# Sums and weighted values of a block's last four heads, issued in two pairs instead of all four at once

## What is computed

```
x = x + block0(group_norm(x))    # q, k, v: 3x3 depthwise convolution, layer norm per head
x = x + block1(group_norm(x))    # q, v get a low-rank term; no convolution
# in each block, for each of 12 heads of 16 channels, over 256 tokens:
attn = q @ k.T / 4 + rel_h[:, :, :, None] + rel_w[:, :, None, :]   # (256, 256)
o    = softmax(attn) @ v         # block0: + q before the output projection
out  = o @ w_proj + b_proj
```

## Time and profile before

| | |
|---|---|
| median of 3 runs | 108.78 us (107.95 to 112.67) |
| the profiled execution's own time | 108.68 us |
| its span, first to last instruction | 106.7 us |
| TensorE matmul busy | 97.1 us (91%) |
| TensorE weight loads busy | 70.8 us (66%) |
| VectorE busy | 62.7 us (59%) |
| ScalarE busy | 51.3 us (48%) |
| GpSimd busy | 31.4 us (29%) |

### The profile page before, as it was taken

One profiled execution on the slowest core, in us unless ns is written; L12 is line 12 of the kernel. 1 busy time (PEld: TensorE's weight loads), 2 busy tenths in 40 slices (PEclk: granted clock), 3 DMA queues, 4 the chain that ended last, 5 costly groups with the idle time before them and its releaser, 6 DMA issues.

```text
span 106.7 us, 2097 instructions
## 1 busy us (share of the span) xinstructions
PE 97.1 (91%) x822; PEld 70.8 (66%) x825; DVE 62.7 (59%) x134; ACT 51.3 (48%) x115; POOL 31.4 (29%) x46
## 2 busy tenths in 40 slices
PE   5799999999959999999999999899989999999780
PEld 2155787578848986777856563797759879857440
DVE  3469995587999667834650135464796493560130
ACT  4011904663534981837815624254246668715820
POOL 8947600599999999000000000000000000000000
PEclk9995579999999999999999999999999999999999
DMA  2999980000000000000000000000000000000002
GB/s 59 308 307 292 237 79 0 3 0 6 0 0 0 9 0 0 0 0 6 0 0 0 0 6 0 0 0 0 0 0 6 0 0 6 0 0 0 0 0 74
DMA packets 2826, 3.73 MB, mean 35 GB/s; under 512 B 305, under 2 KB 2242, under 8 KB 2818
## 3 DMA queue, kind: packets, MB, share of 16 engines
q0 software_dynamic: 784, 0.79, 6.7%
q1 hardware_dynamic: 1282, 1.41, 4.8%
q10 hardware_dynamic: 752, 1.42, 4.5%
HBM read 3.42 MB, written 0.20 MB: 34 GB/s over the span
## 4 chain that ended last, share of the span: by engine, by line
PE 75%; DVE 10%; ACT 7%; DMA 3%; issue 2%
PE bank L917 9%; PE bank L760 8%; PE bank L853 6%; PE bank L850 6%; PE bank L749 6%; PE bank L892 5%; PE bank L905 5%; PE bank L866 5%; PE bank L893 4%; PE bank L831 3%; ACT pt L386 3%; DVE taps_m L622 3%; DMA x<-x_t 3%; PE bank L734 3%; PE bank L832 2%
## 5 line engine op out<-in xcount | busy, mean ns | idle before, releaser
L575 DVE TENSOR_REDUCE mx<-bank 128x2 fp32r<-128x512 f32 x24 | 15.0, 682 | 3.2 <-PE bank L866 3.2
L386 ACT ACTIVATE pt<-bank 128x512 f32<-128x512 f32 x24 | 13.0, 594 | 3.6 <-PE bank L893 3.4
L892 PE MATMUL bank<-qs,ks 128*128 128x256 f32 x48 | 13.3, 310 | 0.8 <-ACT pt L386 0.7
L570 DVE SCALAR_TENSOR_TENSOR qs<-qs,vec,bank 64x512 fp32r<-64x512 f32 x12 | 8.8, 737 | 6.9 <-ACT qs L376 6.8
L893 PE MATMUL bank<-mt,nhot_r 128*128 128x256 f32 x48 | 12.0, 280 | 0.0
L892 PEld LDWEIGHTS bank<-qs,ks 128*128 128x128 f32 x48 | 9.0, 187 | 2.8 <-ACT pt L386 1.8
L760 PE MATMUL bank<-pad,taps_m 128*128 128x256 f32 x36 | 10.5, 445 | 0.2 <-DVE taps_m L622 0.2
L734 PE MATMUL bank<-warm 128*128 128x512 bf16 x28 | 9.0, 443 | 1.5 <-POOL warm L279 1.3
L324 POOL TENSOR_SCALAR tap_p<-pad,vec 64x256 f32<-64x256 f32 (+1 forms) x11 | 10.3, 937 | 0.0
L749 PE MATMUL bank<-xn,w 96*128 96x256 f32 (+1 forms) x40 | 9.6, 428 | 0.6 <-DVE xn L549 0.6
L376 ACT ACTIVATE qs<-bank 64x512 fp32r<-64x512 f32 x12 | 7.1, 590 | 6.2 <-PE bank L853 6.2
(11 more groups left out here) (103 smaller groups left out, 166.7 us busy)
## 6 DMA issues: line engine op xcount, KB each, us to landing
ks<-hots POOLq DMA_DIRECT2D x1, 768.0 KB, 7.8
wp<-w_proj ACTq DMA_DIRECT2D x1, 576.0 KB, 8.1
w<-w_qkv SPq DMA_DIRECT2D x1, 432.0 KB, 8.8
w<-w_qkv SPq DMA_DIRECT2D x1, 288.0 KB, 4.8
cst<-consts ACTq DMA_DIRECT2D x1, 256.0 KB, 4.8
nhot<-neg_hot ACTq DMA_DIRECT2D x1, 256.0 KB, 5.7
x<-x_t SPq DMA_DIRECT2D x1, 192.0 KB, 3.3
wpq<-w_proj_q ACTq DMA_DIRECT2D x1, 192.0 KB, 8.9
```

The source lines that it names most:

```text
L386: act.activation(pt[:, h, :, :], key_banks[h % 2][:, :].rearrange("p (k n) -> p k n", k=QT), ACT.Exp).then_inc(exped[b], 1)
L575: dve.tensor_reduce(mx[:, h, :], ring_bank(h // 4, 4 + h % 4)[:, :].rearrange("p (q n) -> p q n", q=QT), AXX, ALU.max).then_inc(maxed[b], 1)
L892: pe.matmul(dst, ks[:, h, k * 128:(k + 1) * 128], qs[:, h, :], start=True, stop=False)
```

## The change

TensorE's last stage no longer waits for all four exponentials before the sums. `direct_sums` and this call of `weigh` go; in their place `pair_sums` and `pair_weigh` do the same matmuls for two of the four heads (pair 0: j = 0, 1; pair 1: j = 2, 3), each waiting for the exponentials of its own pair. The order after the scores is: weighted values and sums of pair 0, output projection of group 1, sums and weighted values of pair 1, output projection of group 2. In block 0 `q_project(1)` moves up between the scores of the second and third head. On ScalarE the reciprocals of group 1 move ahead of the four exponentials.

```diff
             def last_stage(b):
                 copy_maxima(b, HG - 1)
+                group_tail(b, HG - 2)
                 for j in range(4):
                     exponentials(b, 4 * (HG - 1) + j)
-                group_tail(b, HG - 2)
                 group_tail(b, HG - 1)
...
-            def direct_sums(b, g):
-
-                pe.wait_ge(exped[b], 4 * g + 4)
-                pe.wait_ge(zeroed, 3)
+            def pair_sums(b, g, pair):
+
+                pe.wait_ge(exped[b], 4 * g + 2 * pair + 2)
+                if pair == 0:
+                    pe.wait_ge(zeroed, 3)
                 for k in range(QT):
-                    for j in range(4):
+                    for j in (2 * pair, 2 * pair + 1):
                         mm = pe.matmul(sum_ps[g][32 * j:32 * j + 32, :], ones[:, 0:32], pt[:, 4 * g + j, k, :],
                                        start=(k == 0), stop=(k == QT - 1), skip_group_check=True)
-                mm.then_inc(summed[b], 1)
+                if pair == 1:
+                    mm.then_inc(summed[b], 1)
+
+            def pair_weigh(b, g, pair):
+
+                pe.wait_ge(exped[b], 4 * g + 2 * pair + 2)
+                if pair == 0:
+                    pe.wait_ge(v_set[b], 2)
+                for k in range(QT):
+                    for j in (2 * pair, 2 * pair + 1):
+                        mm = pe.matmul(o_ps[g][32 * j:32 * j + 32, :], va[:, k, 4 * g + j, :], pt[:, 4 * g + j, k, :],
+                                       start=(k == 0), stop=(k == QT - 1), skip_group_check=True)
+                if pair == 1:
+                    mm.then_inc(weighed[b], 1)
...
                 score_by_key(b, 4 * g)
                 score_by_key(b, 4 * g + 1)
+                if b == 0:
+                    q_project(1)
                 score_by_key(b, 4 * g + 2)
                 score_by_key(b, 4 * g + 3)
-                if b == 0:
-                    q_project(1)
-                direct_sums(b, g)
-                weigh(b, g)
+                pair_weigh(b, g, 0)
+                pair_sums(b, g, 0)
                 out_project(b, 1, 0)
                 out_project(b, 1, 1)
+                pair_sums(b, g, 1)
+                pair_weigh(b, g, 1)
                 out_project(b, 2, 0)
                 out_project(b, 2, 1)
```

## The result

| | before | changed |
|---|---|---|
| median | 108.37 us (107.79 to 112.67, 4 runs) | 114.48 us (112.87 to 115.98, 4 runs) |
| ratio | | 1.043, 95% interval 1.028 to 1.058 |
| median, second measurement | 110.00 us (108.60 to 112.17, 12 runs) | 114.18 us (113.56 to 114.89, 4 runs) |
| its ratio | | 1.036, 95% interval 1.029 to 1.043 |
| first profiled execution, span | 106.7 us | 113.6 us |

The change makes the kernel slower by about 4%. The predicted time was 113.0 us, with a range of 111.7 to 114.3: the forecast of a ratio of 1.039 lies inside both intervals, while the median of the first four runs, 114.48, lies 0.2 us above the range's upper end. Two of these four executions, the profiled one among them, were in a slower state (115.58 and 115.98 us) that the ratio leaves out; the other two took 112.87 and 113.39 us.

What follows compares the result with a forecast made beforehand. From the last exponential on, TensorE's own work was taken to set the end. Block 1's +1.93, block 0's +2.38 and 0.05 us for ScalarE made 4.36 us, on 108.68 us: 113.0 us, range 111.7 to 114.3.

Steps and rivals of the forecast that it cites:

- What bounds the stage: End of block 1: from 99.75 us on, TensorE's sums (1.07 us), weighted values (0.86) and projections (1.91) set the end.
- A call on two tiles takes four steps: Pair calls: 8 records on two column tiles take four steps, as long as the full call of 16.
- Rivals 1 and 2: A pair call takes two steps, 110.5 us (chance 0.12); a group of two steps at 0.17 us, 111.9 us (0.04).
- Both stages' sums: Last stages: block 1 +1.93 us and block 0 +2.38 us.
- Why it takes 16: Last stages: each pair call takes four steps, so a stage's narrow work grows from 8 steps to 16.
- The cover of the chain: Group 1's projection, which covered group 2's slog, srec and on, is spent before them; TensorE waits 1.0 us for on.
- q_project: Block 0: moved between the scores, it makes the third head's scores 0.74 us late.
- ScalarE: Group 1's reciprocals fit the 0.83 us idle before the first exponential; 0.02 to 0.03 us charged per block.
- Rival 3: Reciprocals do not fit in front; exponentials start 0.42 to 0.8 us later in both blocks: 113.9 to 114.6 us (chance 0.04).
- rival 4: The clock falls in the new pause, where TensorE waits 1.0 us for on (chance 0.03).

Runs made afterwards that it cites:

- steps: Kernel before, with block 0's last weighted values issued 16 more times, on four, two or one column tiles; 124.17 us in its one run.
- pairs_together: Changed kernel with both projections of group 1 behind all pair calls; last stages +0.59 us (block 0) and +0.13 us (block 1) against before.
- proj_first: Kernel before with group 1's reciprocals ahead of the exponentials and its projections ahead of the whole sums; last stages +0.86 us (block 0), -0.07 us (block 1).
- q_moved: Kernel before with q_project(1) between the scores of the last group's second and third head; last stages +0.48 us (block 0), 0.00 (block 1).
- one_between: Changed kernel with only half of group 1's projection between the pairs, the other half behind pair 1; ratio 1.032, last stages +1.94 and +1.49 us.

## Why the prediction was right, and where its reason was not

- **What bounds the stage** was read rightly: from the fourth exponential on TensorE's own records set the end, so work moved ahead of it counts in full.
- **A call on two tiles takes four steps**: right, 1.06 us for 8 records, and steps shows it for each number of tiles. Rivals 1 and 2 fall: a group of two, four or one has the same step of 0.216 us here.
- **Both stages' sums**: block 1 +1.93 predicted and +1.92 measured, block 0 +2.38 and +2.38. The changed kernel does take 16 steps in each stage. The whole time, 113.0 us, came out less well (114.48 and 114.18 us by the two medians): it was added to one execution of before, and the kernel before itself took 108.37 us in one measurement and 110.00 in the other. The ratios are what bears the forecast out.
- **Why it takes 16** was only half right. "The narrow work of a stage grows from 8 steps to 16" was put down to the pairs. Pairs on different tiles run beside each other when nothing wide stands between them: without the projection there, the cost of the whole change is 0.72 us (pairs_together), not the 2.4 that the same reasoning gave. The rows held the sign: the projections of the earlier trace rows issue both k of the first 64 columns, then both k of the second, and still ran two at a time. The prediction used their length and missed their order. That the count of 16 held is luck as far as this step goes: the change happens to put a wall exactly between its pairs.
- **The cover of the chain**: right. TensorE waits 0.60 us for `on` by the profile's account in both blocks. proj_first prices it alone: 0.86 us in block 0, and nothing in block 1, where the pause pays it back.
- **q_project**: 0.74 us late scores were predicted, and the score starts 0.74 us later. Alone it costs 0.48 (q_moved).
- **ScalarE**: 0.05 us were charged, 0.00 measured. Rival 3 falls.
- **The clock** (rival 4): the pauses for `on` ran at a granted clock of 1.00 (60 to 68 us and 106 to 111 in the first profile), and no stretch at 0.50 came directly behind block 0. One, 3.41 us long, came 17.7 us later in the first profile and added 1.4 us; no run shows what one directly behind block 0 would cost. By its letter the prediction's sign, "a slice of PEclk at 5 behind block 0", is there, but the 4.3 us are there without it: the second profile of the same kernel had none. Why the clock falls there in some executions, and whether an idle TensorE at the end of block 0 has a part in it, stays open; no run here was made to tell.

## What to carry to other kernels

Narrow matmuls on column tiles cost here by the fullest tile: a step of 0.216 us took one record on each tile in use, whether four, two or one were (steps). So splitting a call that fills all tiles into calls that fill half of them saved nothing, 1.06 us for 8 records against 1.07 for 16, unless calls for the other tiles stood next to them in the program (pairs_together: 16 records in 1.07 us); in steps a tile came at most four steps early. One matmul of 96 columns between them made the halves run one after the other (one_between: 8 records in 1.03 us on one side of it, 8 in 1.06 on the other). And before work is moved into a pause, look at what it covers now: here the projection hid three serial steps of two other engines.

## What the runs showed that was not expected

Column tiles of TensorE run ahead of each other across calls, against program order: in pairs_together the sums of pair 1 started in the same step as the first sums of pair 0, 0.2 us after the exponential that they waited for, with all four steps of pair 0's sums still to run. In steps `weigh` started four steps, 0.86 us, ahead of the end of the calls in front of it. The lead was bounded, at two steps and at four: tile 1 stood free for 12 steps in that run before the calls on tiles 0 and 2 let it in. An estimate from these leads (two and four steps in steps, four in pairs_together, with two steps to a matmul) is that each tile holds one matmul that waits beside the one that runs, and that everything behind keeps its order; no run was made to test it.
